# Second feed-forward of a two-layer decoder: turning interleaved with the second product of the tile before, later addition, statistics on ACT

## The reference, cut to what matters

```python
def _act_quant(x):
    scale = 127.0 / jnp.clip(jnp.max(jnp.abs(x), axis=-1, keepdims=True), 1e-05)
    return jnp.clip(jnp.round(x * scale), -128.0, 127.0) / scale
def _weight_quant(w):
    scale = 1.0 / jnp.clip(jnp.mean(jnp.abs(w)), 1e-05)
    return jnp.clip(jnp.round(w * scale), -1.0, 1.0) / scale
def _bitlinear(x, w):
    return jnp.einsum('bsd,fd->bsf', _act_quant(x), _weight_quant(w))
h = jax.nn.silu(_bitlinear(x, W1))            # 512 -> 2048
x = _layernorm(x + _bitlinear(h, W2))         # 2048 -> 512, mean and variance over 512
```

## Time and profile before

| | us |
|---|---|
| median of three executions | 3282.03 |
| the profiled execution | 3278.3 |
| its span | 3276.6 |
| first product of tile 0 in the second feed-forward | at 3100.25 |
| end of the last statistics | at 3258.29 |

### The profile page before, as it was taken

The page is one execution under the profiler, slowest core; times in us unless marked ns, Lnnn a source line. Parts: engine busy times, 40 slices in busy tenths (PEclk is TensorE's granted clock), DMA queues, the critical chain, the costliest instruction groups (busy, mean ns, idle before and its releaser), DMA issues. The chain is left out here.

```text
span 3276.6 us, 80440 instructions
## 1 busy us (share of the span) xinstructions
PE 2951.4 (90%) x29987; PEld 2015.7 (62%) x30006; DVE 2576.6 (79%) x4692; ACT 2401.8 (73%) x6066; POOL 1950.9 (60%) x2266
## 2 busy tenths in 40 slices
PE   7999887736899999999999999999999999997386
PEld 5666555514566666666676666766766667665243
DVE  4555568885788888888888888888888888886796
ACT  4444343435888888888888888888888888886554
POOL 1111166504877777788777787787877878774000
PEclk9999998968999999999999999999999999999699
DMA  5110043401010110101101011010110101100201
GB/s 219 40 33 27 20 146 108 139 10 58 21 34 21 47 34 23 38 21 47 34 21 40 21 46 34 21 41 21 40 41 21 41 21 36 45 21 1 103 1 52
DMA packets 63473, 146.50 MB, mean 45 GB/s; under 512 B 8704, under 2 KB 17536, under 8 KB 59904
## 3 DMA queue, kind: packets, MB, share of 16 engines
q1 hardware_dynamic: 63104, 141.53, 13.8%
HBM read 128.06 MB, written 13.45 MB: 43 GB/s over the span
## 5 line engine op out<-in xcount | busy, mean ns | idle before, releaser
L2153 DVE TENSOR_TENSOR delta_Pb<-delta_bank,delta_lev 128x512 f16<-128x512 f32 x448 | 310.4, 693 | 148.6 <-PE delta_bank L2482 148.6
L2145 DVE SCALAR_TENSOR_TENSOR delta_F<-delta_bank,delta_cw,delta_F 128x510 f32<-128x510 f32 (+1 forms) x512 | 381.5, 745 | 42.8 <-ACT delta_far L1955 28.7
L2456 PE MATMUL delta_bank<-delta_xh,delta_qkvh 128*128 128x512 f16 x1024 | 390.1, 381 | 6.9 <-DVE delta_F L2145 4.5
L2456 PE MATMUL delta_bank<-delta_xl,delta_qkvh 128*128 128x512 f16 x1024 | 389.2, 380 | 0.0
L2456 PE MATMUL delta_bank<-delta_xh,delta_qkvl 128*128 128x512 f16 x1024 | 388.7, 380 | 0.0
L1695 POOL TENSOR_TENSOR delta_F<-delta_F,delta_far 128x506 f32<-128x506 f32 x256 | 278.4, 1088 | 93.4 <-DVE delta_F L2145 93.4
L1675 POOL TENSOR_SCALAR_AFFINE_SELECT delta_LA<-delta_LA 128x512 f32<-128x512 f32 x128 | 81.5, 637 | 376.3 <-DVE delta_LA L2183 355.4
L2170 DVE CAST delta_XT<-delta_bank 128x512 f16<-128x512 f32 x384 | 262.8, 684 | 50.4 <-PE delta_bank L2501 47.3
L2441 PE MATMUL delta_bank<-delta_zh,delta_xh 128*128 128x256 f16 x1024 | 279.3, 273 | 0.6 <-ACT delta_gz L1977 0.6
L2441 PE MATMUL delta_bank<-delta_zh,delta_xl 128*128 128x256 f16 x1024 | 279.2, 273 | 0.0
L2441 PE MATMUL delta_bank<-delta_zl,delta_xh 128*128 128x256 f16 x1024 | 278.9, 272 | 0.0
(11 more groups left out here) (375 smaller groups left out, 10171.3 us busy)
## 6 DMA issues: line engine op xcount, KB each, us to landing
delta_Gb<-g_rows SPq DMA_DIRECT2D x64, 512.0 KB, 5.3
conv_wf<-in_W SPq DMA_DIRECT2D x72, 256.0 KB, 3.4
delta_st_qkv<-in_Wqkv SPq DMA_DIRECT2D x17, 1024.0 KB, 8.4
conv_T<-filters SPq DMA_DIRECT2D x32, 256.0 KB, 3.4
delta_st_zo<-in_Wz SPq DMA_DIRECT2D x16, 512.0 KB, 8.1
delta_st_zo<-in_Wout SPq DMA_DIRECT2D x16, 512.0 KB, 6.6
conv_ahead_C<-in_ctx_rev SPq DMA_DIRECT2D x1, 6144.0 KB, 27.7
ternary<-conv_spare SPq DMA_DIRECT2D x36, 128.0 KB, 2.8
```

Of the source, the lines that this page charges most:

```text
L2145: ve.scalar_tensor_tensor(dst, src, cw_tap(i, 3 - lag), dst, ALU.mult, ALU.add)\
L2153: ve.tensor_tensor(left(Pb[:, lvl, :, :], lvl), comp(bank[5], lvl), bc(lev[:, lvl, :].rearrange("p (n s) -> p n s", s=1 << lvl), 1, 8), AL ...
L2456: ins = te.matmul(bk[:, :], ww[:, QKV[job], kc, :], xx[:, kc, tok:tok + 512], start=(m == 0), stop=(m == 11))
```

## The change

1. PE: in turn t, the four groups of turning of h of tile t-1 alternate with the four quarters (four products each) of the second product of tile t-2. The second product of a tile is thus a turn later. Its first quarter waits for the addition of tile t-3.
2. DVE: the addition in turn t is that of tile t-4 (before: t-2), and stands between quantise_x and quantise_h. `moments` is gone from DVE.
3. ACT: `moments` of tile t-5 at the end of turn t: an Identity with its sum, a Copy that makes the negative mean, a Square with the mean as bias and its sum. The last norm takes the negative mean and the sum of squares: three of its instructions have another form.

```diff
-            for t in range(NT + 1):
+            def moments(t):
+                act.wait_ge(g["add"].sem, g["add"].at(1, t))
+                if t >= 1:
+                    act.wait_ge(g["st"].sem, g["st"].at(3, t - 1))
+                s_.activation(junk[:, 0, :], X[:, t, :], ACT.Identity, accum_out=total[:, t:t + 1])\
+                    .then_inc(g["st"].sem, 1)
+                act.wait_ge(g["st"].sem, g["st"].at(1, t))
+                s_.activation(mv[:, t, 0:1], total[:, t:t + 1], ACT.Copy, scale=-1.0 / D).then_inc(g["st"].sem, 1)
+                act.wait_ge(g["st"].sem, g["st"].at(2, t))
+                s_.activation(junk[:, 1, :], X[:, t, :], ACT.Square, bias=mv[:, t, 0:1], accum_out=mv[:, t, 1:2])\
+                    .then_inc(g["st"].sem, 1)
+
+            for t in range(NT + 5):
...
+                if t >= 5:
+                    moments(t - 5)
...
-            for t in range(NT + 2):
+            for t in range(NT + 4):
                 if t + 1 < NT:
                     quantise_x(t + 1)
-                if 0 <= t - 1 < NT:
-                    quantise_h(t - 1)
-                j = t - 2
-                if j >= 1:
-                    moments(j - 1)
+                j = t - 4
                 if j >= 0:
                     dve.wait_ge(g["m2"].sem, g["m2"].at(1, j))
                     ve.scalar_tensor_tensor(X[:, j, :], bank[7][:, :], tok[:, 1, j:j + 1], X[:, j, :], ALU.mult,
                                             ALU.add).then_inc(g["add"].sem, 1)
-            moments(NT - 1)
+                if 0 <= t - 1 < NT:
+                    quantise_h(t - 1)
...
                 j = t - 1
-                if 0 <= j < NT:
-                    pe.wait_ge(g["hq"].sem, g["hq"].at(2, j))
-                    for n in range(4):
+                k = t - 2
+                for n in range(4):
+                    if 0 <= j < NT:
+                        if n == 0:
+                            pe.wait_ge(g["hq"].sem, g["hq"].at(2, j))
                         if n >= 2:
                             pe.wait_ge(g["hc"].sem, g["hc"].at(n - 1, j))
...
+                    if 0 <= k < NT:
+                        if n == 0 and k >= 1:
+                            pe.wait_ge(g["add"].sem, g["add"].at(1, k - 1))
+                        if n == 0 and k == 0:
+                            pe.wait_ge(ahead.loaded["W2"].sem, ahead.loaded["W2"].at(1))
+                        pe.wait_ge(g["hc"].sem, g["hc"].at(n + 1, k))
+                        for c in range(4 * n, 4 * n + 4):
+                            last = te.matmul(bank[7][:, :], hqT[:, k % 2, c, :], w2q[:, c, :], start=(c == 0),
+                                             stop=(c == FC - 1))
+                        if n == 3:
+                            last.then_inc(g["m2"].sem, 1)
...
-            ve.tensor_scalar(var[:, :], mv[:, :, 1], 1e-5, None, ALU.add).then_inc(variance.sem, 1)
+            ve.tensor_scalar(var[:, :], mv[:, :, 1], 1.0 / D, 1e-5, ALU.mult, ALU.add).then_inc(variance.sem, 1)
...
-            ve.scalar_tensor_tensor(nb[:, :], mv[:, :, 0], -1.0, rs[:, :], ALU.mult, ALU.mult)\
-                .then_inc(shift.sem, 1)
+            ve.tensor_tensor(nb[:, :], mv[:, :, 0], rs[:, :], ALU.mult).then_inc(shift.sem, 1)
             for i in HALVES[1]:
-                ve.tensor_scalar(X[:, i, :], X[:, i, :], mv[:, i, 0:1], rs[:, i:i + 1], ALU.subtract, ALU.mult)\
+                ve.tensor_scalar(X[:, i, :], X[:, i, :], mv[:, i, 0:1], rs[:, i:i + 1], ALU.add, ALU.mult)\
                     .then_inc(by_dve.sem, 1)
```

More of the change, by code:

```diff
@@ L1168, in ffn1_stage @@
         h = sb("h", [P, 2, FF])
-        st = sb("st", [P, 2, 6])
+        total, junk = sb("total", [P, NT]), sb("junk", [P, 2, D])
         hq = sb("hq", [P, 2, FF], BF16)
@@ L1172, in ffn1_stage, with turned_h @@
         g = {n: counter(n, c) for n, c in dict(
-            ib=1, mx=1, inv=3, x1=2, xt=1, xc=1, m1=4, sl=4, st=1, mo=1,
+            ib=1, mx=1, inv=3, x1=2, xt=1, xc=1, m1=4, sl=4, st=3,
             hx=1, hs=3, hq=2, ht=4, hc=4, m2=1, add=1).items()}
         block = ctx.enter_context(nc.Block())
+        def turned_h(n):
+            return bank[5 + n % 2][:, 0:256]
         @block.gpsimd
@@ L1210, in _ @@
                 j = t - 1
-                if j >= 0:
+                if 0 <= j < NT:
                     for n in range(4):
@@ L1216, in _ @@
                         s_.activation(hqT[:, j % 2, 4 * n:4 * n + 4, :].rearrange("p a b -> p (a b)"),
-                                      bank[5 + n % 2][:, 0:256].bitcast(BF16), ACT.Copy).then_inc(g["hc"].sem, 1)
+                                      turned_h(n).bitcast(BF16), ACT.Copy).then_inc(g["hc"].sem, 1)
+                if t >= 5:
+                    moments(t - 5)
         @block.vector
@@ L1318, in _ @@
                             c = 4 * n + i
-                            last = te.transpose(bank[5 + n % 2][:, i * 64:(i + 1) * 64].bitcast(BF16),
+                            last = te.transpose(turned_h(n)[:, i * 64:(i + 1) * 64].bitcast(BF16),
                                                 hq[:, j % 2, c * P:(c + 1) * P], ib[:, :])
                         last.then_inc(g["ht"].sem, 1)
[L1322 to L1332, removed]
+                    if 0 <= k < NT:
[9 more added lines that the diff above has]
+                            last.then_inc(g["m2"].sem, 1)
 NKH, NVH, DK = 16, 32, 128
```

## The result

The changed kernel takes 3269.52 us (median of nine, 3264.53 to 3272.36), the kernel before, measured beside it, 3278.84 (median of nine): 9.3 us less. The ratio is 0.9965, with a 95% interval from 0.9955 to 0.9975, so it is faster by more than the 0.2% that can be told from no change. The forecast was 10.2 us less, from 3282.03 to 3271.8.

The account below looks back on a forecast made before the run. TensorE's waits in the turning bound the loop at 9.55 us a tile; 16.8 us won up to the tail, less a tail of 13.8 instead of 7.2, gives 10.2: 3282.03 to 3271.8 us, range 3266.5 to 3278.0.

Parts of the forecast that it names:

- What bounded the kernel: Second feed-forward loop: the chain TensorE, Silu, TensorE with waits in the turning holds a tile at 9.55 us.
- The interleaving: TensorE's turn: quarters of the second product cover ACT's copies, the 1.09 us wait and its partner go, leaving 8.00 us.
- my upper bound of 0.2 us a tile: TensorE: six more changes between turning and products per tile, taken at 0, at most 0.03 us each.
- The statistics on ACT: End of ACT's turn: 1.70 us a tile against DVE's 0.82, hidden ahead of the fourth Silu with 0.24 to spare.
- The addition of t-4: TensorE's quarter 0 waits for DVE's addition behind quantising x: 16.62 us for two turns, 8.31 a tile.
- The head: Loop start: first products of turns 3 and 4 (s_3, s_4) begin at 3123.66 and 3133.52.
- The tail: After the last quantised h: 13.8 us instead of 7.2, ACT's queue of five statistics ending last.
- The sum: Whole change: end of last statistics from 3258.3 to 3248.1, so 10.2 us less, median 3271.8.
- The first (turns of 8.00): Loop: the two-turn chain doesn't bind and 8.00 a tile holds, 3.7 us more saved, 3268.1; chance 0.12.
- The second (ACT late): ACT: statistics at 2.4 us delay the fourth Silu, 3278.1; with all small drags 3275.5 to 3279; chance 0.17.
- The third (tables): ACT: Identity or Square needs other tables than Silu, two loads of 1.28 us a tile, 3287; chance 0.03.
- The fourth (the clock): TensorE's clock falls to 1.2 GHz at head or tail: four tiles 3299, chance 0.05; one tile 3278.7, chance 0.03.

## Why the prediction was right, and by how much it was off

**What bounded the kernel.** Right: TensorE with its waits in the turning. The kernel before with DVE relieved kept its 9.55, and the changed kernel without the interleaving went back to it.

**The interleaving.** Right: 1.09 and its smaller partner are gone. From quarter 0 to the next first product it is 4.13 us (3159.79 to 3163.92) against the forecast 4.11, so a change between turning and products costs next to nothing, and my upper bound of 0.2 us a tile was not needed.

**The statistics on ACT.** 1.70 us forecast, 1.70 measured. The room ahead of the fourth Silu was mis-sized: 0.24 forecast, 0.42 by the run with two more copies. I had given the copy ahead its whole record of 0.60 where the next instruction starts after 0.49, and Silus in a row start 0.57 apart, not 0.59. The rule of the Trainium skill that I weighed (ScalarE: Activation LUTs, "Rules for kernel authors", additions on VectorE) gives the right price order here, 1.70 against 0.82. But what decided is where room is: in the kernel before the move costs 0.9, in the changed one it brings 1.7.

**The addition of t-4.** This step carried the forecast and held: two turns 16.67 (8.64 + 8.03) against 16.62. Moved ahead of quantising x, the addition lets the turn fall to 8.02.

**The head.** s_3 and s_4, shifted by the 2.94 that this run is ahead, were to be 3120.72 and 3130.58; they are 3120.73 and 3130.59.

**The tail.** 14.1 against the forecast 13.8. The mis-sized term is the statistic in a queue, 1.81 forecast and 1.90 measured (Squares at 3237.35 and 3239.24, 1.89): the next Identity starts 0.09 after the reading of the sum ends, and I had put 0.01 (0.83 for a Square whose record with its reading is 0.82).

**The sum.** 9.60 in the stretch against 10.2. Of the missing 0.6, 0.27 are the 0.05 of each of the two-turn rounds, and the rest is the tail. The medians moved by 9.3. That the measured 3269.52 is 2.3 under the forecast 3271.8 though less was won is luck of the starting point: the kernel before measured 3278.84 beside it, not 3282.03.

**Rivals.** The first (turns of 8.00) would have come true with the other place of the addition. The second (ACT late) needs more than the 0.42 us that ACT has to spare. The third (tables) did not occur: there is no table load between the Silus and the statistics. The fourth (the clock) did not occur in the profiled execution of the changed kernel. In the runs it did, once in the tail, for 3.5 us and at a price of 1.5 where I had put 6.9 for a whole tile, and five times at the head of the loop, where it was hidden. I had given 0.08 to a fall that costs a tile or more. A fall came in six of the eight runs, but only one of the six cost anything; what decides it stays open.

## What to carry to other kernels

When engines work in turns, follow each wait that the change adds once round through all engines and divide by the number of turns that it spans: work per turn said 8.00, the round said 8.31, and the chip 8.33. A software pipeline that is made deeper pays its depth again at the end, here 6.9 us of 16.5 that the loop had won (tail 14.1 against 7.2), and the order at that end is worth work of its own. Among instructions of one engine, put first the one that another engine waits for.

## What the runs showed of the hardware that I had not expected

TensorE's clock: an idle time of 1.83 us, four transposes and 0.27 idle left it at 1.00 in the changed kernel and in three runs with the same tail; 2.46 us, four transposes and 0.26 idle were once followed by 0.54 for 3.5 us, at a price of 1.5 us. But in five other runs it fell to 0.50 after waits of only 1.06 and 0.47 us with turning between them, while the same rows left it at 1.00 in the kernel before, in the changed one and in three runs. One difference ahead of it is on record: in those five the clock had risen to 1.00 some 3.5 us ahead of tile 1's first product, in the others 1.8 to 2.5 us. So the length of a gap by itself doesn't tell whether the clock falls; what does wasn't tried.

An instruction of ACT with a sum has a record of its own for reading the sum (0.19 us). The next instruction that doesn't need it starts before that record ends (Square at 3164.73, Silu at 3165.45, 0.72 as in the earlier trace rows); one that waits for it starts 0.09 after the end. So five statistics in a row cost 1.90 each, and one ahead of a Silu 1.70.
